# A four-layer perceiver on one core: the identity products in front of TensorE's waits are taken out

## What is computed

```python
x = x + _L0_xattn_ref(_layernorm(x), ctx_1024, ...)      # mean of the context
x = x + _L0_attn_ref(_layernorm(x), ...)                 # causal linear attention, 16 heads
x = x + _L0_ffn_ref(_layernorm(x), ...)                  # 8 experts, best 2
x = x + _L1_xattn_ref(_layernorm(x), ctx_1024, ...)      # one similarity to all context rows
x = x + _L1_attn_ref(_layernorm(x), ...)                 # causal softmax attention, 16 heads
x = x + _L1_ffn_ref(_layernorm(x), ...)                  # quantised weights
x = x + _L2_xattn_ref(_layernorm(x), ctx_1024, ctx_1024, mask, ...)  # 16-head attention over the context
x = x + _L2_attn_ref(_layernorm(x), ...)
x = x + _L2_ffn_ref(_layernorm(x), ...)                  # 8 experts, best 2
x = x + _L3_xattn_ref(_layernorm(x), ctx_1024, mask, ...)            # 16-head attention over the context
x = x + _L3_attn_ref(_layernorm(x), ...)                 # decayed recurrence
x = x + _L3_ffn_ref(_layernorm(x), ...)                  # 8 experts, dispatched by capacity
```

## Time and profile before

| | |
|---|---|
| three executions | 1592.42, 1596.67, 1596.86 us (median 1596.67) |
| the profiled execution | 1588.98 us, its span 1587.2 us |
| TensorE busy | 1508.6 us (95%) |
| VectorE, ScalarE busy | 973.9 us (61%), 954.2 us (60%) |
| mean granted TensorE clock | 0.992 |

### The profile page before, as it was taken

One profiled execution on the slowest core, in us unless ns is written; L12 is line 12 of the kernel. 1 busy time (PEld: TensorE's weight loads), 2 busy tenths in 40 slices (PEclk: granted clock), 3 DMA queues, 4 the chain that ended last, 5 costly groups with the idle time before them and its releaser, 6 DMA issues.

```text
span 1587.2 us, 33990 instructions
## 1 busy us (share of the span) xinstructions
PE 1508.6 (95%) x13838; PEld 1107.0 (70%) x13838; DVE 973.9 (61%) x1860; ACT 954.2 (60%) x1453; POOL 9.7 (1%) x22
## 2 busy tenths in 40 slices
PE   6999999899999999999998999999999999998899
PEld 5766587667677767777776666777777777776664
DVE  5523323657777688776775325776767676767631
ACT  3121042238887888887883214887777777778711
POOL 0000000000000000000000000000000000000000
PEclk9999999799999999999999999999999999999999
DMA  9576855264535353444312466443434343323346
GB/s 392 235 282 262 303 195 213 83 234 178 177 113 173 134 201 119 152 152 149 114 45 114 174 236 227 146 168 119 153 117 153 115 154 117 141 94 109 131 180 270
DMA packets 56165, 270.81 MB, mean 171 GB/s; under 512 B 6608, under 2 KB 6864, under 8 KB 49360
## 3 DMA queue, kind: packets, MB, share of 16 engines
q1 hardware_dynamic: 56016, 268.70, 46.3%
HBM read 161.33 MB, written 4.59 MB: 105 GB/s over the span
## 4 chain that ended last, share of the span: by engine, by line
PE 80%; DVE 8%; issue 5%; ACT 5%; DMA 2%; POOL 0%; SPq 0%; DVEq 0%; ACTq 0%
PE T L852 14%; PE O L875 9%; PE S L838 8%; PE O L852 7%; PE T L810 6%; PE T L823 5%; PE S L680 5%; PE O L1005 3%; PE O L810 3%; PE S L1158 3%; PE O L1187 3%; PE T L675 2%; PE O L823 2%; ACT sc L1273 2%; DVE sc L1703 2%
## 5 line engine op out<-in xcount | busy, mean ns | idle before, releaser
L1703 DVE CUSTOM_DVE_ANT_0 sc<-S,mask_bias,small 128x896 f32<-128x896 f32 x336 | 377.6, 1149 | 46.8 <-PE S L838 46.8
L1273 ACT ACTIVATE sc<-sc,small 128x1792 f32<-128x1792 f32 x168 | 300.1, 1786 | 2.6 <-DVE small L1703 1.0
L1259 ACT ACTIVATE pT<-T 128x512 f32<-128x512 f32 x366 | 212.2, 597 | 87.2 <-PE T L852 87.2
L852 PE MATMUL T<-consts,sc 128*128 128x128 f32 x1546 | 232.7, 281 | 5.0 <-ACT sc L1273 3.1
L875 PEld LDWEIGHTS O<-pT,arena 128*32 128x32 f32 x6272 | 164.9, 110 | 74.8 <-issue 72.3
L852 PEld LDWEIGHTS T<-consts,sc 128*128 128x128 f32 x1546 | 168.9, 141 | 60.9 <-issue 39.7
L875 PE MATMUL O<-pT,arena 128*32 128x128 f32 x6272 | 194.4, 274 | 9.0 <-ACT pT L1259 9.0
L838 PE MATMUL S<-keys,q 64*128 64x512 f32 (+1 forms) x896 | 151.3, 415 | 10.1 <-DVE small L1703 9.9
L1669 DVE COPY pT<-T 128x512 f32<-128x512 f32 x150 | 103.6, 690 | 79.2 <-PE T L852 78.5
L1259 ACT ACTIVATE pT<-O 128x512 f32<-128x512 f32 x194 | 115.9, 597 | 52.4 <-PE O L852 52.4
L810 PE MATMUL T<-ctx_in,packs 128*128 128x448 f32 x320 | 133.4, 541 | 1.1 <-issue 1.1
(11 more groups left out here) (368 smaller groups left out, 1830.2 us busy)
## 6 DMA issues: line engine op xcount, KB each, us to landing
keys<-keys_hl SPq DMA_DIRECT2D x224, 448.0 KB, 4.5
ctx_in<-in_ctx_cols SPq DMA_DIRECT2D x46, 896.0 KB, 5.2
wide<-in_ctx_rows SPq DMA_DIRECT2D x14, 896.0 KB, 4.6
wide<-in_up_L0f SPq DMA_DIRECT2D x8, 1408.0 KB, 8.0
sc<-in_ctx_cols SPq DMA_DIRECT2D x10, 896.0 KB, 5.6
wide<-in_up_L2f SPq DMA_DIRECT2D x8, 1024.0 KB, 6.6
wide<-in_down_L2f SPq DMA_DIRECT2D x8, 1024.0 KB, 4.8
wide<-in_up_L3f SPq DMA_DIRECT2D x4, 2048.0 KB, 9.2
```

Of the source, the lines that this page charges most:

```text
L852: last = nc.tensor.transpose(ring(plan, u)[:, t * P:(t + 1) * P], weights_of(2 * m + i)[:, b * P:(b + 1) * P], ident)
L1259: nc.scalar.activation(pT2[:, g * BANK:(g + 1) * BANK], ring(plan, u), ACT.Copy).then_inc(s["t_act"], 1)
L1273: nc.scalar.activation(weights_of(n), weights_of(n), ACT.Exp, bias=n_best[c % 2][:, h:h + 1], scale=-1.0, accum_out=l_new[c % 2][:, h:h + ...
L1703: V.tensor_tensor_reduce(weights_of(n)[:, i * HC:(i + 1) * HC], S4f[:, n % 2 * 2 * BANK:n % 2 * 2 * BANK + HC], mask_bias[:, i * HC:(i + 1 ...
```

## The change

`warm` does nothing any more. All its 30 calls stay in the code and issue no instruction:

```diff
             def warm(bank, n):
 
-                for _ in range(n):
-                    mm(bank[:, 0:P], ident, ident, start=True, stop=True)
+                return None
 
             def early(of, b, bank, free=0):
```

## The result

The changed kernel takes 1610.4 us (median of four executions, 1608.46 to 1611.86) against 1595.72 us before (the three executions shown above and a fourth, 1594.77). The two medians stand 14.7 us apart, a quotient of 1.0092; the record's estimate from all executions is a ratio of 1.0106, 95% interval 1.0085 to 1.0127. So the change makes the kernel slower, by about 1%. Its profiled execution took 1609.1 us, its span 1607.3; against the profiled execution of before (1588.98, 1587.2) that is 20.1 us.

What follows compares the result with a forecast made beforehand. TensorE at its higher clock was taken to bound the kernel nearly everywhere. Clock costs of 21.5 us less 6.0 gained gave +15.5; 1 us off, added to the 1596.67 median, gave 1611 us (77%), range 1602 to 1621.

Steps and rivals of the forecast that it cites:

- rival B: Everywhere: only unbroken idle time lowers the clock, the few products left keep it up; 1595 us, 7%.
- Rival C: At the five late waits: late groups bind, the clock doesn't follow or its falls cost little; 1591 us, 5%.
- L1x's two: Before L1x's first transposes and at L1x's end: late identity groups removed, gaining 1.33 and 1.44 us.
- L1a: Head products: 1.61 us gained from a late group, 0.9 us lost as first results come at half clock.
- L1f: Transposes of xn and of y1: late groups removed, gaining 0.7 and 0.63 us.
- line 1113: Its 32 16-column records in L3a take about 7 us instead of 3.75 at half clock, costing 3.2 us.
- the last place: L3x's tail, L3a and start of L3f: clock falls to 0.50, costing 8.6 us.
- the start of L1x: Clock falls to 0.50; slower transposes 0.25 us and wide work behind 2.0 us, costing 2.25 us.
- likewise where L0a hands over to L0f: L0a's tail into L0f: clock expected at 0.50 there too, costing 3.2 us.
- The two falls given one half and one third: L1x into L1a, clock fall given one half, 1.2 us; L1f into L2x, given one third, 0.7 us.
- L3x's start: L2f into L3x: little work left, clock falls to 0.50, costing 2.25 us.
- The step from the profiled execution to the median: Whole kernel: 1 us off for falls already present before, so 14.5 us added to the 1596.67 us median.

## Why the prediction was right, and which terms were off

**The bound and the mechanism** held. The clock fell in all places that I had given it, in both that I had called uncertain and in one that I hadn't named (L0a's head products, below). In the run with narrow products it stayed at 0.50 while TensorE was busy 42.99 of 44.30 us, and the loss came all the same, so rival B is out. Rival C (the late groups bind) had the gain right, as the run without late products shows, but the price of the falls wrong.

**The gains.** In the ledger L1x's two gave 1.3 us each for 1.33 and 1.44. L1a gave 0.5 net for 0.7 and L1f 0.9 for 1.3.

**The costs at half clock** were read from rows and came out as read: line 1113 +3.2 predicted, 6.98 − 3.75 = 3.2 found; the last place 8.6 against 8.0; the start of L1x 2.25 against 2.1.

**L0a was undersized**: 3.2 predicted, 5.6 found. The failing step is "likewise where L0a hands over to L0f", counted from the tail on. In the order of time of the kernel after:

```profile
60.78 5.37 PE L789 MATMUL S<-pT,arena 128*128 128x512 f32 x8 [2.87 <-DVE pT L1542]
```

The clock fell once at 62.2 us, 1.4 us into these products and behind the wait of 2.87 us ahead of them, and they were slow for it; VectorE, which takes their results, fell back 1.7 us. At 68.99 it fell again, for 13.6 us. No narrow product stands ahead of the first fall, only that wait between two groups of wide work. The run that keeps only the last six calls falls here too, and the one with 16-column products in this wait doesn't.

**The two falls given one half and one third** (L1x into L1a 1.2, L2x 0.7) both came: 1.7 and 1.5 us. **L3x's start** cost 2.75 us for 2.25.

**The step from the profiled execution to the median was wrong**, and 1611 met 1610.4 so closely by luck. The sum on the profiled execution was 15.5 us, and 20.1 were found. For the median I took 1 us off, for falls that other executions of the kernel before may have had anyway. Measured against the four executions of before (1595.72), that term should have been about 5: they lie 6.7 us over the profiled one, the changed kernel's only 1.3 over its own. Part of it is real. The run without the last six calls has the clock at 0.50 at 68 and 955 us in code that is the same, and 7.35 us lost; what has already fallen can't fall again, so the change costs such an execution less.

But the base was high as well. The 34 later executions of the kernel before, on two chips, have medians of 1591.09 (13) and 1591.75 us (21), only 2 to 3 us over the profiled one. Against those the changed kernel's 1610.4 us is a loss of about 19 us, close to the 20.1 of the traces. The forecast thus started from a median of three executions that lay some 5 us high, and added costs that were 4.6 us short, and the two cancelled. Whether those first executions were high by chance or by the chip they ran on, the record doesn't say. With 20.1 us in place of 15.5 and the same base the forecast would have been 1616, still in the range.

Not settled: whether an execution falls at such a half-filled place. At 955 us the run without the last six calls did, and the kernel before didn't in its trace, with the same instructions ahead and the same wait of 2.60 us.

## What to carry to other kernels

Dummy products in a wait are worth what wide work stands behind the wait, so price each place: what follows at half clock, until the clock is back, against how late the last dummy ends. Fill a wait with wide products, but end them before what is waited for; in the ledger this change was a loss of some 24 us and a gain of some 4, and taking the late products out alone got the gain without the loss. And a profiled execution is one draw: a kernel with half-filled waits has a spread, and its best execution is the wrong ground for a sum.

## What the runs showed that I had not expected

- Widening a head product costs no time here: each record, with a 128-column weight load, takes 0.114 us with 17 and with 119 columns. The mean clock was a little higher with the wide ones.
- The same narrow records follow the clock: 0.117 us at 1.00, 0.21 to 0.22 at 0.50, though they stream only 16 columns. So narrow fillers can do double harm: at most places they didn't hold the clock, and once it is low they end late.
- Identity products cut the spread of the executions from about 10 us to 3.0 us, but only once the half-filled waits are filled too.
